# A one-core transformer kernel whose order of work is planned ahead: longer landings in the plan, and a new order

## The reference

```
x = x + 0.5 * ffn(layernorm(x))      # layer 1
x = x + attention(layernorm(x))      # layer 2
x = x + 0.5 * ffn(layernorm(x))      # layer 3, same weights as layer 1
```

## Time and profile before

| | |
|---|---|
| runs | 508.12, 509.01, 515.56 us |
| the profiled execution | 504.51 us, of which the span is 502.3 us |
| PE busy | 464.7 us (93%) |
| DVE busy | 347.1 us (69%) |
| POOL busy | 285.3 us (57%) |
| ACT busy | 272.2 us (54%) |

### The profile page before, as it was taken

How to read it: one execution, slowest core, us unless ns; L and a number is a source line. 1 busy time by engine, 2 the same in 40 slices (tenths; PEclk the granted TensorE clock), 3 DMA queues, 4 the chain that set the end, 5 groups by cost and what they waited for, 6 DMA issues and landing times.

```text
span 502.3 us, 9736 instructions
## 1 busy us (share of the span) xinstructions
PE 464.7 (93%) x2975; PEld 385.6 (77%) x2975; DVE 347.1 (69%) x1064; ACT 272.2 (54%) x612; POOL 285.3 (57%) x290
## 2 busy tenths in 40 slices
PE   7998799999999999999999999999898989989967
PEld 4777677887788887887878779778787877877756
DVE  4898587333668865889998799998877523545434
ACT  5955124555566756667554756655365555465410
POOL 4238355565666445644766657686565456656650
PEclk9999899999999999999999999999999999999997
DMA  8981212344431233321133322114343343552313
GB/s 227 370 289 43 84 64 89 99 144 133 111 90 64 78 112 106 101 65 37 64 102 85 89 71 78 49 53 116 81 138 110 95 141 107 152 142 69 91 47 90
DMA packets 74353, 53.68 MB, mean 107 GB/s; under 512 B 9664, under 2 KB 68928, under 8 KB 74304
## 3 DMA queue, kind: packets, MB, share of 16 engines
q1 hardware_dynamic: 66112, 36.26, 24.5%
q0 software_dynamic: 8192, 16.79, 11.0%
HBM read 26.87 MB, written 26.15 MB: 106 GB/s over the span
## 4 chain that ended last, share of the span: by engine, by line
PE 69%; DVE 12%; issue 8%; ACT 5%; another core or an unknown queue 2%; DMA 1%; SPq 1%; POOL 1%; DVEq 0%; ACTq 0%
PE pool L894 16%; PE pool L883 7%; PE gu L851 7%; PE gu L849 7%; PE gu L850 6%; PE pool L906 5%; PE gu L808 4%; PE gu L810 3%; PE gu L809 3%; PE pool L832 3%; DVE hs L1225 1%; DVE X L1248 1%; ACT gs L1039 1%; PE pool L922 1%
## 5 line engine op out<-in xcount | busy, mean ns | idle before, releaser
L1182 POOL DMA_INDIRECT yg<-y_sorted,places x128 | 124.0, 968 | 92.5 <-PE gu L851 34.2
L1162 POOL DMA_INDIRECT x_sorted<-xn,places x128 | 131.6, 1028 | 78.1 <-issue 35.3
L1225 DVE TENSOR_TENSOR hs<-gs,gu 128x512 f32<-128x512 f32 x92 | 60.9, 663 | 76.2 <-ACT gs L1039 52.3
L1039 ACT ACTIVATE gs<-gu 128x512 f32<-128x512 f32 x124 | 72.2, 583 | 75.9 <-PE gu L810 33.3
L894 PE MATMUL pool<-w,hT 128*128 x708 | 98.6, 282 | 7.7 <-ACT hT L1045 4.7
L894 PEld LDWEIGHTS pool<-w,hT 128*128 128x128 f32 x708 | 87.3, 191 | 22.0 <-issue 19.0
L849 PE MATMUL gu<-w,xbt_hi 128*128 x177 | 82.1, 464 | 0.3 <-issue 0.2
L1045 ACT ACTIVATE hT<-pool 128x512 f32<-128x512 f32 x92 | 53.2, 580 | 35.5 <-PE pool L883 28.5
L851 PE MATMUL gu<-w,xbt_hi 128*128 x177 | 70.0, 395 | 0.0
L850 PE MATMUL gu<-w,xbt_lo 128*128 x177 | 69.9, 395 | 0.0
L1020 ACT ACTIVATE ys<-pool 128x256 f32<-128x256 f32 x92 | 34.5, 376 | 64.2 <-PE pool L894 51.8
(11 more groups left out here) (132 smaller groups left out, 812.3 us busy)
## 6 DMA issues: line engine op xcount, KB each, us to landing
xb<-x_sorted SPq DMA_DIRECT2D x85, 128.0 KB
y_sorted<-ys SPq DMA_DIRECT2D x85, 128.0 KB
x_sorted<-yg SPq DMA_DIRECT2D x6, 512.0 KB, 7.1
X<-x_dram SPq DMA_DIRECT2D x8, 256.0 KB, 4.8
x_sorted<-xn,places POOLq DMA_INDIRECT x128
yg<-y_sorted,places POOLq DMA_INDIRECT x128
out_dram<-X SPq DMA_DIRECT2D x8, 256.0 KB
raw<-gate_w_dram SPq DMA_DIRECT2D x4, 256.0 KB, 4.6
```

What stands on the lines that cost most here:

```text
L1039: nc.scalar.activation(dst, src, ACT.Silu).then_inc(silu_done, 1)
L1162: nc.gpsimd.indirect_dma_start(x_sorted[g], bass.IndirectOffsetOnAxis(places[g][:, k, t:t + 1], 0), xn[:, b, t % T], None).then_inc(scatte ...
L1182: nc.gpsimd.indirect_dma_start(yg[slot][:, k, t], None, y_sorted[g], bass.IndirectOffsetOnAxis(places[g][:, k, at:at + 1], 0)).then_inc(ga ...
L1225: v.tensor_tensor(hs[n % HB][:].rearrange("p (j i) -> p j i", j=2)[:, 0:k], gs[n % GB][:].rearrange("p (j i) -> p j i", j=2)[:, 0:k], bank ...
```

## The change

All four `lands` of moves, loads and stores are raised: scatters and gathers from 200 to 320, loads and stores from 190 to 310. The string `URGENCY` is replaced as a whole, so that every engine's order is new. And a front with a single half now waits, in the plan and in the kernel, for both reads of the unit two before it. No operation is added or taken away, and all shapes, buffers and groups stay.

```diff
@@ -39,24 +39,24 @@
 URGENCY = (
-    "HPP]OPc}]ZPIXXhGLHQLbTiP^FACPHNFN?K>Ea<F7]9-NB`HTdKP@.D>IZdGReJF=QH8H@XB;VOgWQ_ZP%JIXPTQgPRRPI`SS9HWOa##5Y`f7O"
+    "QGYQN=CLaJN[>3O_NNOPKSyLaN<>OK-]@LDN^JRON{eRN*OVOUF[0A<`PG>.OPlRLETS#L}C4P-NxKLQJY@lPFZUJRSSFW#HMISPHJ7SCA;ANP"
...
@@ -212,7 +212,7 @@
-            op(("scatter", g, n), "POOL", 126, ("place", g), *free, ("norm", *GROUPS[g][n // 2 // T], 1), lands=200)
+            op(("scatter", g, n), "POOL", 126, ("place", g), *free, ("norm", *GROUPS[g][n // 2 // T], 1), lands=320)
@@ -220,7 +220,7 @@
-                op(("gather", l, b, n), "POOL", 126, *done, lands=200)
+                op(("gather", l, b, n), "POOL", 126, *done, lands=320)
@@ -232,7 +232,7 @@
-        op(("load", r), "SP", 47, *scattered, back("pair_turn", XB), lands=190)
+        op(("load", r), "SP", 47, *scattered, back("pair_turn", XB), lands=310)
@@ -245,7 +245,7 @@
-        op(("store", r), "SP", 47, ("y_copy", r), lands=190)
+        op(("store", r), "SP", 47, ("y_copy", r), lands=310)
@@ -408,7 +408,7 @@
-                single = u[0] == "R" and width(*self.pair[u[1]]) == 1
+                single = ("front", u, 1) not in ops
@@ -416,7 +416,10 @@
-                return after(self.freed(n - 2)[j]) if n >= 2 else 0
+                if n < 2:
+                    return 0
+                times = [after(k) for k in self.freed(n - 2)[0 if single else j:2 if single else j + 1]]
+                return None if None in times else max(times)
@@ -837,6 +840,8 @@
                 if nth_unit[u] >= 2:
                     once.wait_ge(*freed(nth_unit[u] - 2)[j])
+                    if ("front", u, 1) not in plan.ops:
+                        once.wait_ge(*freed(nth_unit[u] - 2)[1])
```

More of the change, by code:

```diff
@@ L57 @@
-    "<MeXNR9W7LP%RHHQaB5UFPOYPNHL_O1OPNTC;OmZCL:QOSU6wAJ}Oq,QQ8[NhZESAA@KaMr>iL[gDYB8PTS<hNS>xBPVK`Ibq}SSkLb.GSJV6^"
-    "PQnLb#R;-QeFKg}OH1>QISP`+NMd#*KP[?QKh$@}IB]6ZOUW_JVhL]=IwPLHgVLdOW-O]`E9ULNicRBCM@RZ.@gJ>Xs4PXSd]KBBEWE-IY)z:U"
-    "HLSKYD>IOZ]PPP@F*IGP8YZMCQFT^LAUG>Vf)PX<CWJF-XQWNPUaRFbUXaTK")
+    "QGYQN=CLaJN[>3O_NNOPKSyLaN<>OK-]@LDN^JRON{eRN*OVOUF[0A<`PG>.OPlRLETS#L}C4P-NxKLQJY@lPFZUJRSSFW#HMISPHJ7SCA;ANP"
+    "URVKOXTUKNVHUFPOqt?2MC>WKT^XQmTwKTjI=5UPOhM_`WX=Ms96FCGn9^WJ`U<3PSNeLRLETYKGVQPjHEHNPTX,DTHQpNT@F:NHVS@nJN^MWU"
@@ new lines @@
+    "2QZNFPLHtRP[;GE#dEWPHIf9>ObMGVP]8LODQL8<U^Q*P[XFSPPJHKETE=7T.H?PPLYnAL_S>`QURiT6IhML;:JPQ`FROMTQ=ZdQPbJMMPGa3a"
+    "h>PPM[F#z8CFXZGOd6PrIlEPMGSD3KAPgYSOJ]UHDP>8A&LUNTP^eMQ#*7OG9UURPNR`#RDOZII^dH_L;7NP?WNb@Ov>NPQPSPP<JqPlDWOZ]("
+    "=SFSPDaXY@WIP`=SbOL#>dRPH]2AMOaPTP8G7H]HPFNBj[IkE^U^UNZG>FLGfb^ji`AR7<gN<,WAJUkZ$SdjIQP[@PYUL5M@><NLSeNVFJQ)=;"
+    "NUQlX:McXNX=VPFZCZbsBaP@aKFJE;OMPQGPEPKN#`JY8KQUmiTRBO8UPTPYI@K^S_e_evKKVNXYqXsTGSyfoV]G{_t5K;IBPN^>KO]NXkRP=o"
+    "P`1ULYRSHWJUKLHW[IRRRTH^YFVlhYWUM^_GG@@aFg2FK>E2ROSKDSILCIWPNe,QOARYH^GL}eneTH_K^RhUnVZXPGQL}GLPMPbPVPk}wu}i=c"
@@ new lines @@
+    "kmvXnnTPSUH|TMKrCXIP_@bVIQeEy//@U[c`@>VZ5O4=BL[0GFSEVQNVcbv[E@ISLRNVUdM>B6`a#PeH;a[UVOjXBGR`XgTm4a;S[;.[GRURRP"
+    "ZDKA?YPYOY<ZLOGKGP@<iYBUQP?P?KP;rVP@AI[OZKPFPZDFZKPj?D3U[]rLQ_h_%8MhXE^N>N]ILJ6bPIRQRN]GLKHKPViUSOsRRW/TYM3W_Z"
+    "EKXYCiPJjUPXPIW;P?P.JHWFzPX.XNASPcPXZSSB+GUrETQDMMX,B@UM>bd_TOOwLE3aQSFSQO%WD_0fIN_W`PgaVWP:NN]hPP<FPV#fKLMd^J"
+    "<EZS=;J[v_lO06UNMHA[S]UTRNP2LBS@<M?@_KDC3Y@QcqOfKDLRXB#RUWWGV`XJcGRQNInOWAYEZXY>[R@>VNTVYOPPOnNITJW?[cBb@PiLAG"
+    "OzWaCC?PG=TPY?M]TQPPa>JR6`Uj>[^NPTQLZUJP`UR>^hXBKNWXHIPUP]QQI3VOj7K%GMCGP<PLcPEOWl9`OWiP?XZiAP9NPRXETpOBL=NLDG"
@@ new lines @@
+    "ERV_JQDP^Z1I`P8SQJBH?L4YFPCXEYWpcQ`sPI<PIKTTS[RHXHOV<QN$W}Jn[;JR:MaN:^mK?M?PEWT@QPIdB:>PG[NPMG`^SPPLZPKL`QbaHP"
+    "=YRNB(PWOYESVPUP?PZMUn[lOPr[QNC+Qe>FNPPULaLP9If?hYlP;QakVY_ZQIcfBVPMI._JbF}icWKZUQXLfpcOg]NLWI[N_S}In[?^NCZN}P"
+    "RiIRRHI?4`TZbz@aW]PL%C4h_j6kUHPPOdjZPc=bY4B@_GBTLDf_QR#CP@SBjKc]PTg[TPcP^PlB`oPQ#_fjMUgrb.OP@MP^OPPPYa}c*6IW*["
+    "7l^KyF;PYPKbOkJPW8PNCSkRIb_VWNAcE[PiTTD`eJI@ILrlej8[OCJZMPe><Tb[QSPJEPPXqT=PPQ]PRDPSdKdgkMhMKWN>Kb:2^U7@GL]zfh"
+    "bKXQ/DNMY]_hUKXcAWOUTBB}UXXPXP@BR]j?tT]Xe.;8U>`Y]dJ}f=FMN-PUVNHj4O@:VPsB-K36WBNU%rNu|?JDRNWORRCV_BXPSO0[>_+qVM"
@@ L60 @@
+    "P2l6`4HsD`e<R?;Q23aQm8Sr>@.RKJtH]AuhW[H=QHoOaQnVNReT`w<PPJ^i")
 BLANK = 2 * T * D
```

## The result

| | before | with the change |
|---|---|---|
| runs, us | 508.12, 508.91, 509.01, 515.56 | 520.60, 521.49, 522.12, 522.18 |
| median | 508.96 | 521.81 |
| profiled execution (span) | 504.51 (502.3) | 522.18 (520.0) |
| PE busy, idle in the span | 464.7, 37.6 | 468.2, 51.8 |

The ratio is 1.026, with a 95% interval of 1.021 to 1.030: slower by 12.9 us. The forecast was 505 us, with a range of 497 to 516. Against the profiled execution of before it is 17.7 us, 14.2 of it idle time of PE and 3.5 longer matmuls.

The account below looks back on a forecast made before the run. PE was taken as the bound, busy 464.7 of 502.3 us. From the profiled 504.5 us, 0.1 (pair 12) and 3.9 (end) came off, giving 500.5; adding 4.5 us for the runs' median gave 505 us, range 497 to 516.

Parts of the forecast that it names:

- The opening: PE's stop before `count`, behind `chosen` and `xt_lo`: no gain in the likeliest case, 6.5 us if it does not recur.
- 3.5 us unchanged: Sign that the prediction is right: PE's idle time of 3.5 us in the opening stays as it was.
- Pair 12, -0.1 us: First pair of group 1: PE waits for ACT's copy instead of the DMA; gain 0.1 us, at most 0.5 us.
- The end, -3.9 us: Last stretch: two more fronts cover a late release of `sdown`; net gain 3.9 us, at most 5.0.
- under 1.5: Sign that the prediction is right: PE's longest idle time at the end stays under 1.5 us.
- a loss, 1.7 us: At the end, ACT and DVE work without PE work beside it; 1.7 us lost, net, if no late release mattered before.
- The 1.3 us ahead of the last `sdown`: Sign that the prediction is right: about 1.3 us of PE idle time there, at the end.
- All else, zero, 4 us either way: 20.0 us of small waits over the middle 400 us, dealt anew: no sign expected, 4 us either way.
- The expected cut of PE's busy time by 2 us: Sign that the prediction is right: PE's busy time over the kernel falls by some 2 us.
- The second: Rival, no net change: late release moves elsewhere or plain runs never had it; 1.7 us loss, 511 us; 25%.
- The third: Rival, slower through DVE in the attention: six more operations there, 3.7 us, plus slow clock and end loss; 517.5 us; 16%.
- The landings: Planned load 2.51 to 3.71 us, gather 3.40 to 4.60; old figures already right or long, no instruction gets longer.

Follow-up runs that it names:

- fourth chip: Follow-up set on another chip: the kernel before took 473.05 us, the changed kernel, run once more unchanged, 479.86 us, ratio 1.014.
- the splice of the first 80 us: The change's order for all that starts in the first planned 80 us, the order before for the rest: 473.59 us, 1.001 to the kernel before.
- the splice of the end alone: The order before up to 385 planned us, the change's order for the rest: 474.39 us, 1.002 to the kernel before.
- the first set: The follow-up runs made on the second chip: three with the pause and one splice of the two orders, ratios 0.999 to 1.021 to the kernel before.
- the pause: Changed kernel with small memsets on POOL, each waited for, behind group 0's 16 scatters: 513.37 us, 1.011; behind every scatter and gather: 516.15 us, 1.015.
- second chip: Chip of the first set, where the kernel before took 512.09 us.

## Why the prediction was wrong

Where each order stands, by the start of DVE's low part of a pair (us; the last column is the span):

| | pair 0 | 12 | 28 | 56 | 91 | end |
|---|---|---|---|---|---|---|
| first chip, before | 70.3 | 110.5 | 176.6 | 350.0 | 466.4 | 502.3 |
| first chip, changed | 79.2 | 124.7 | 192.1 | 371.1 | 487.0 | 520.0 |
| lost so far | 8.8 | 14.1 | 15.5 | 21.1 | 20.7 | 17.7 |
| fourth chip, before | 62.6 | 101.4 | 165.8 | 334.1 | 442.2 | 470.7 |
| fourth chip, changed | 66.5 | 104.7 | 168.9 | 340.0 | 448.0 | 478.1 |
| lost so far | 3.9 | 3.3 | 3.1 | 6.0 | 5.9 | 7.4 |

A pair may stand earlier or later among the other work in a new order, so a column is a rough mark of progress: at pair 0 the changed kernel is 3.9 us behind on the fourth chip, while the splice of the first 80 us costs half a microsecond there.

1. **"The opening: nothing is gained in the likeliest case", "3.5 us unchanged": wrong, and the first failed step.** The chain of instructions was indeed the same, but I had taken the stop for a property of the chain. It was 7.59 us. It goes with the row of scatters beside it: 10 in a row, turn to copy 6.0 us; 12 in a row, 10.7 us; spaced, none. The number of moves does not set it alone, since behind the 10 gathers in a row at the old end the longest delay was 3.3 us. I had priced nothing on POOL.
2. **Pair 12, -0.1 us: the mechanism right, the price wrong on the first chip.** The turn no longer waits for a transfer, and PE waits for ACT's copy at `down`. By the rows of before that was 0.3 to 0.4 us, and on the fourth chip, without late releases, it is 0.37 us:

```profile
102.78 1.15 PE L899 MATMUL pool<-w,hT 128*128 x8 [0.37 <-ACT hT L1050]
```

   On the first chip it is 4.45 us, behind 6 scatters in a row. The new order has put nothing between `hidden_turn` and `down` that would cover a late release.
3. **The end, -3.9 us: nearly right, in part by luck.** From the low part of pair 91 to the end it takes 33.0 us instead of 35.9, 2.9 us less; the slow clock is gone, and PE goes on without a wait where the old stop of 4.01 us was (behind the two `sdown` at 501.06). But I had let the release come as late as before, and had counted on longer cover alone. In the trace the longest delay there is 1.9 us instead of 3.3, and POOL's longest row is 6 moves instead of 10, so the gain can't be put to the cover. The longest idle time is 2.37 us, not under 1.5. Without late releases I had forecast a loss, 1.7 us; it is 1.6 us by the traces of the fourth chip (30.1 against 28.5) and 0.8 us by the splice of the end alone. The 1.3 us ahead of the last `sdown` are 1.41 us there.
4. **"All else, zero, 4 us either way": wrong, and the second failed step.** The idle time from 75 to 475 us grew by 9.6 us. Two stops beside rows (3.31 us, and 4.45 where 0.51 was) make 7.3 of it, and 2.4 us are left. On the fourth chip, without late releases, the idle time of the same part grew by 2.0 us (8.4 from 75 to 445 us, against 6.5 from 75 to 440), since PE waits more for DVE's `hid` and low parts. That is not the whole price of the new order there: by the splices the part from 80 to 385 us costs 1.15%, 5.4 us, and longer busy time of PE is in it. The expected cut of PE's busy time by 2 us became a rise of 3.5, and of 3.0 on the fourth chip. I had no row from which this could be priced, and gave a zero where only a range was known.
5. **The rivals.** The second ("the late release finds another place") named the thing, but let it only move, never grow, and so got 511 us. The third named DVE, by way of full DVE in the attention; DVE was busy less there, not more. What happened is the wait for `hs` without that cause. Its 517.5 us lies 4 us under the measured 521.8, but it is made of other terms, so the nearness is luck. The two were given a quarter and a sixth as alternatives; the waits that each spoke of came together.
6. **The landings: right.** The counts, tiles and wait that they bring cost 0.0 to 0.5% with the old order. No transfer is named ahead of more PE work than before. The Trainium skill ("DMA: Bandwidth & Descriptors", anatomy of one DMA on the gpsimd path) gives about 2.0 us plus the bytes over 436 GB/s, an estimate of 2.15 us for a gather of 64 KB. On the page of the profile of the changed kernel from the fourth chip the median from issue to landing is 2.6 us, so the trace lies a fifth above the estimate.
7. **Whose is the late release?** I cited the Trainium skill ("Perfetto Trace Analysis", summary of the profiler window per engine type), by which the profiler's end of a TensorE instruction is an estimate. The late releases agree with it in so far as a release stood up to 10.7 us behind that end. The trace speaks against PE being late itself: in the changed kernel PE starts a front at 48.45, 0.1 us behind the `hid` on DVE that it needed, while the release of a turn that stood before it comes at 58.9. Four overdue releases arrive within 0.3 us of each other, and no release of DVE or ACT is late; that looks like releases of PE that were held up together, but it is an argument and not a test. How long matmuls can wait behind their record is not shown, and this stays open.

Shown: the first stop goes when the scatters are spaced; releases are late in every trace of the first comparison and of the first set, and in none of the four sets after it; 1.4% belongs to the order, most of it (1.15%) between 80 and 385 us. Argued: that the stops at 76.4 and 117.3 us on the first chip are of the same kind (the one at pair 12 shrank under the pause, in one trace). Also argued: that late releases make the other half of the 12.9 us, which sets one chip against another. Open: what differs between the sets, the chip or the time; whether descriptors or bytes matter; and what the pause is worth, since the changed kernel was not itself run on the second chip, so that the 1.5% won by it compares two chips. A part of the events is missing as well: the traces with late releases hold 536 to 565 events of PE, the others 679 to 683, so their counts and delays are lower bounds.

## What to carry to other kernels

A stop whose releaser the profile can't name is not a fixed cost of the chain that it stands in: look at what else runs during it, count it, and ask whether the change makes that longer. Between orders found by search, "all else" is not zero: an order that is new everywhere lost 1.4%, by small waits and longer matmul time that no single row forecasts. And compare two kernels on more than one chip, and at more than one time, before explaining a per cent: the same kernel took 509 to 512 us in two comparisons and 473 us in the four after them.
